# A transformer block (half feed-forward, attention, half feed-forward) on eight cores: two small jobs move from ScalarE to VectorE, and one dependency of the gate/up matmuls is split in two

## What is computed

```
x = x + 0.5 * ffn(layernorm(x))
x = x + attn(layernorm(x) * g + b)
x = x + 0.5 * ffn(layernorm(x))

ffn(x):  gate = x @ Wg.T;  up = x @ Wu.T          # 1024 -> 3072, int weights / 127
         return (silu(gate) * up) @ Wd.T          # 3072 -> 1024
attn(x): q, k, v = x @ Wq + bq, x @ Wk + bk, x @ Wv + bv   # 16 heads of 64
         w = softmax(q k^T / 8);  return w @ v
```

## Time and profile before

| | us |
|---|---|
| median of 2 runs | 4691.66 |
| the two runs | 4689.4 and 4693.92 |
| the profiled execution | 4682.5 |
| its span, slowest core (core 0) | 4681.0 |
| spans of the 8 cores | 4652.3 to 4681.0 |

### The profile page before, as it was taken

How to read it: one execution, slowest core, us unless ns; L and a number is a source line. 1 busy time by engine, 2 the same in 40 slices (tenths; PEclk the granted TensorE clock), 3 DMA queues, 4 the chain that set the end, 5 groups by cost and what they waited for, 6 DMA issues and landing times. The chain is left out here.

```text
span 4681.0 us, 55973 instructions; the slowest of 8 cores (4652.3 to 4681.0 us)
## 1 busy us (share of the span) xinstructions
PE 3372.0 (72%) x21982; PEld 1599.4 (34%) x22214; DVE 940.8 (20%) x1454; ACT 1504.1 (32%) x1864; POOL 145.0 (3%) x307
## 2 busy tenths in 40 slices
PE   0000997976866677589798897986876677579799
PEld 0000443432323343344343443432323344334344
DVE  1101113114320111121221212213330111131221
ACT  0001111101029999711110111101019999721110
POOL 1011000010000000000000000010000000000000
PEclk9999998987988998889899898997888988889899
DMA  8996232232000111123221232213000111033221
GB/s 226 207 260 168 69 121 80 56 80 73 9 18 1 37 37 37 65 63 117 81 72 73 72 117 81 72 48 87 28 18 1 37 37 37 23 95 117 81 73 44
DMA packets 344400, 353.90 MB, mean 76 GB/s; under 512 B 84552, under 2 KB 281160, under 8 KB 343120
## 3 DMA queue, kind: packets, MB, share of 16 engines
q1 hardware_dynamic: 238160, 230.74, 16.9%
q0 software_dynamic: 30976, 100.68, 6.8%
q10 hardware_dynamic: 75008, 18.88, 3.6%
HBM read 255.89 MB, written 88.08 MB: 73 GB/s over the span
## 5 line engine op out<-in xcount | busy, mean ns | idle before, releaser
L900 ACT ACTIVATE att_eS<-PS,cb 128x1024 bf16<-128x1024 f32 x1024 | 1051.1, 1132 | 32.8 <-PE PS L886 31.9
L886 PE MATMUL PS<-Q,K 64*128 64x512 bf16 x2048 | 431.7, 419 | 266.8 <-ACT att_eS L900 175.8
L818 PE MATMUL PS<-V,att_eS 128*128 128x65 bf16 x8192 | 373.2, 203 | 69.8 <-DVE att_x2b L849 69.8
L390 PE MATMUL PS<-ident,a1s_xntm 128*128 128x128 bf16 x256 | 32.4, 306 | 531.1 <-DVE a1s_xntm L377 531.1
L818 PEld LDWEIGHTS PS<-V,att_eS 128*128 128x128 bf16 x8192 | 312.7, 104 | 207.4 <-issue 207.4
L438 PE MATMUL PS<-cs_xnfm,cs_wslg 128*128 128x512 bf16 x1504 | 365.9, 384 | 7.1 <-DVE cs_xnfm L399 5.6
L438 PE MATMUL PS<-a1s_xnfm,a1s_wslg 128*128 128x512 bf16 x1504 | 365.6, 384 | 6.8 <-DVE a1s_xnfm L399 5.3
L444 PE MATMUL PS<-cs_xnfm,cs_wslu 128*128 128x512 bf16 x1504 | 363.0, 381 | 1.7
L444 PE MATMUL PS<-a1s_xnfm,a1s_wslu 128*128 128x512 bf16 x1504 | 362.0, 381 | 1.7
L482 PE MATMUL PS<-a1s_wdsb,a1s_hsb 128*128 128x512 bf16 x1504 | 332.2, 380 | 9.4 <-DVE a1s_hsb L461 7.8
L482 PE MATMUL PS<-cs_wdsb,cs_hsb 128*128 128x512 bf16 x1504 | 330.5, 379 | 9.2 <-DVE cs_hsb L461 7.5
(11 more groups left out here) (109 smaller groups left out, 2074.1 us busy)
## 6 DMA issues: line engine op xcount, KB each, us to landing
a1s_wslg<-wgT SPq DMA_DIRECT2D x48, 512.0 KB, 4.2
a1s_wslu<-wuT SPq DMA_DIRECT2D x48, 512.0 KB, 5.4
cs_wslg<-wgT SPq DMA_DIRECT2D x48, 512.0 KB, 4.1
cs_wslu<-wuT SPq DMA_DIRECT2D x48, 512.0 KB, 5.4
a1s_xst<-L_attn_x SPq DMA_DIRECT2D x32, 512.0 KB, 6.3
x1s<-a1s_xo POOLq DMA_DIRECT2D x32, 512.0 KB, 4.6
a2s_xst<-x1s SPq DMA_DIRECT2D x32, 512.0 KB, 3.4
att_x1q<-x1s SPq DMA_DIRECT2D x8, 2048.0 KB
```

Source lines behind the costliest of these rows:

```text
L390: inst = e.transpose(tview[:, dc * 128:(dc + 1) * 128], xntm[:, (tt % 2) * 1024 + dc * 128: (tt % 2) * 1024 + (dc + 1) * 128], ident[:])
L818: inst = e.matmul(PS1[:, (par * 2 + q2) * 512: (par * 2 + q2) * 512 + 65], expS[:, buf + kt * 1024 + par * 512 + qt * 128: buf + kt * 1024 ...
L886: inst = e.matmul(PS0[:, pp + par * 512: pp + (par + 1) * 512], K_sb[64 * par:64 * par + 64, hp * 2048 + r * 128: hp * 2048 + (r + 1) * 12 ...
L900: "scalar", lambda e, hp=hp, r=r, buf=buf, pp=pp: e.activation(expS[:, buf + r * 1024: buf + (r + 1) * 1024], PS0[:, pp:pp + 1024], AF.Exp ...
```

## The change

Three edits.

1. In `ffn_phase` the steps with th=0 wait for the fourth evacuation of the group, those with th=1 for the eighth, as all did before.
2. In `emit_norms` the 16 squares of a sequence are a product of the chunk with itself on VectorE instead of a Square on ScalarE.
3. In `attn_phase` the copy of the row sums is made by VectorE instead of ScalarE, and a drain is put ahead of the reciprocal that follows it on the same engine.

```diff
-                grp_ev = t_ev[g * 8 + 7]
+                grp_ev_h = {0: t_ev[g * 8 + 3], 1: t_ev[g * 8 + 7]}
...
                             t_mmgu = ph.op("tensor", gu_fn,
-                                           deps=[t_lg, t_lu, grp_ev,
+                                           deps=[t_lg, t_lu, grp_ev_h[th],
                                                  t_silu.get((g, k - 2)),
                                                  t_hmul.get((g, k - 2))],
...
-                t_sq[dc] = ph.op("scalar", lambda e, s=src_sb, dc=dc, sl=sl: e.activation(
+                t_sq[dc] = ph.op("vector", lambda e, s=src_sb, dc=dc, sl=sl: e.tensor_mul(
                     nsq[:, sl * 2048:(sl + 1) * 2048],
-                    s[:, dc * 2048:(dc + 1) * 2048], AF.Square),
+                    s[:, dc * 2048:(dc + 1) * 2048],
+                    s[:, dc * 2048:(dc + 1) * 2048]),
                     deps=[t_mm.get(dc - 2), t_red.get(pi - 1),
-                          t_sq.get(dc - 1)], inc="sc")
+                          t_sq.get(dc - 1)], inc="ev")
...
-                    t_l = ph.op("scalar", lambda e, qtp=qtp: e.copy(
+                    t_l = ph.op("vector", lambda e, qtp=qtp: e.tensor_copy(
                         lbuf[:, qtp * 4: qtp * 4 + 4][:, :, None],
                         PS1[:, :].rearrange("p (a t) -> p a t", a=4)[:, :, 64:65]),
-                        deps=pvdeps, inc="sc")
+                        deps=pvdeps, inc="ev")
                     t_r = ph.op("vector", lambda e, qtp=qtp: e.reciprocal(
                         lbuf[:, 8 + qtp * 4: 8 + qtp * 4 + 4],
-                        lbuf[:, qtp * 4: qtp * 4 + 4]), deps=[t_l], inc="ev")
+                        lbuf[:, qtp * 4: qtp * 4 + 4]),
+                        deps=[t_l], inc="ev", pre_drain=True)
```

## The result

| | before | changed |
|---|---|---|
| ratio of the times, changed to before | | 0.9877 (95% interval 0.9854 to 0.9901) |
| the same on the median shown of before, 4691.7 us | 4691.7 | 4634 (4623 to 4645) |
| two fastest runs, us | 4689.4, 4693.9 | 4634.7, 4638.6 |
| profiled execution, us | 4682.5 | 4621.2 |
| its mean span over the 8 cores, us | 4667.3 | 4599.2 |

The change makes the kernel 1.2% faster, 58 us (46 to 68); the forecast was 56 us, to 4636.

The account below looks back on a forecast made before the run. TensorE bounds the feed-forward stages, ScalarE the attention stages, dependent chains the short stages between. Gains 7 + 17 + 0 + 21 + 12 - 1 = 56 us take 4691.7 to 4636 us, range 4614 to 4668.

Parts of the forecast that it names:

- part 1: Feed-forward gate/up start: no wait for the eighth evacuation, 8 groups x 0.9 us, 7 us gained (3.5 to 10.6).
- if the clock rises at the same moment as before, an earlier start is worth half: Lower end for the gate/up start: matmuls run at the lower clock level, leaving 3.5 us gained.
- Part 2: Norms: squares on VectorE at 1.22 us each, a half falls from 17.26 to 12.96 us, 17 us gained.
- Rival A: Norms: the bf16 product runs at the f32 rate, 12 us lost instead of 17 gained, 4665 us; chance 0.08.
- The table load: Norms: one ScalarE load of 1.30 us leaves the start, one enters ahead of the square root; 0 gained.
- Part 3: Attention: row-sum copy on VectorE, 21 us from ScalarE's queue, 12 from shorter waits, 1 lost beside the residual adds.
- The slots: Attention: ScalarE's queue without the copies, 122 x 0.17 us, 21 us gained.
- the waits: Attention: TensorE gets its PV chunk 0.6 us earlier, so ScalarE waits less at low clock; 12 us gained (0 to 25).
- B: Attention: low-clock stretches end with the gap the copy makes, all 25 us of short waits go, 4623 us; chance 0.12.
- C: Attention: ScalarE's freed time is not used because TensorE then paces, 4668 us; chance 0.11.
- D: Attention: VectorE's chain makes TensorE, then ScalarE, wait at every chunk pair; at a 2.3 us chain 4718 us; chance 0.03.
- Up to 1.73 costs nothing: Attention: a VectorE chain up to 1.73 us makes no ScalarE wait; beyond it each us costs 124 us.

Follow-up runs that it names:

- The filled gap: Kernel before plus three unread matmuls ahead of each group's first gate matmul, old dependency kept: ratio 0.9976 (0.9961 to 0.999).
- part 1 by itself: Kernel before with only the split dependency of the gate/up steps: ratio 0.9983 (0.9946 to 1.002), profiled execution 4666.45 us.
- the last: Changed kernel with first gate/up step among the transposes, reciprocal straight out of PSUM and squares on both engines: ratio 0.9774, runs 4573 to 4579 us.

## Why the prediction came out as it did

**The total and the step that failed.** The total came out close, 58 us measured (46 to 68) against 56, and the change is within 2%, as forecast. It was made of three terms, of which two had about the right size. The third, part 1, is the step that failed: it was forecast at 7 us and measured 15. By the stage times the three add up to 66 us, so a total that fits within 2 us is partly luck.

**Part 1, forecast 7 us, measured 15, above its upper end of 10.6.** What goes is the wait for the eighth evacuation, as the text said; the term was mis-sized in two steps. The first took the gap as 0.9 from the recorded end of the transposes; the next matmuls can start before that end, so 1.22 went. The second was "if the clock rises at the same moment as before, an earlier start is worth half": the clock was let in only as something that lowers the gain. The filled gap shows that the moment moves with the pause, from 5.7 to 2.8 us after the transposes, which is worth 1.36 us a group; part 1 moves it as far (2.9), and as its matmuls also start earlier and so more of them at the low clock, 0.65 a group is left.

**Part 2, forecast 17 us, measured 18 (14.5 by the ratio).** The price of 1.22 for a product not seen before, got by halving the f32 product's part above the fixed 0.16, met 1.225. The Trainium skill (VectorE: DVE Perf Modes, the perf-mode tier table) has 1224 ns for it; the trace agrees. Rival A falls with it. The half for Q came out at 12.62, the one for K at 13.17, where more selector matmuls found the low clock. The table load moved as forecast and cost nothing on balance; the Trainium skill (ScalarE: Activation LUTs, What ACT_TABLE_LOAD costs) counts about 2.66 us with a drain, and the rows have a load of 1.28 from 1393.42 with nothing of a drain to be seen behind it, the root starts at 1394.71. That "by the page's figure the change would give back 1.4 us in each sequence" didn't follow: one load leaves and one enters, at whichever price, and the balance is 0 either way.

**Part 3, forecast 32 us, measured 33.** The slots gave 18 of 21, the waits 14 of 12. The chain was 1.27 against 1.29. One of the things that the text asked the profile to show was misstated, the reciprocal "about 0.9 after the PV chunk's end": by the text's own terms it is 0.44, and it is 0.41 (1480.71 to 1481.12). The text asked for a waiting time near 19 us and it is 15 to 16.

**The rivals.** B (all of the short waits go) and C (the freed time is not used) both fall: the waits went by half. D had half of the mechanism and the wrong price. The chain did not reach its threshold, but a long chain is dearer than stated: at 1.80 it cost 29 to 33 us, where D's reckoning gives 0.07 x 124 = 9, and at 2.59 twice what it gives. "Up to 1.73 costs nothing" asked when ScalarE is late at the high clock, and there it holds nearly. What it left out is that TensorE already waits when its chunk is late against its own place (1.35), and that with those waits the time at the low clock grows, where ScalarE's waits arise. At 1.80 all of part 3 is given back. So a slot freed on ScalarE with a chain about as long as before's brings next to nothing.

**Left open.** Why part 1 by itself measures 8 us by the ratio and 15 by its stage can't be told apart from scatter: its interval reaches from 25 us gained to 9 lost. How much of part 3's halved waits is the clock and how much the earlier chunk wasn't separated by a run; by the table the time at the low clock fell by 28% (225 to 162), and the waits for each us of it by 30% (0.123 to 0.086), so the two seem to share it. Which pauses of TensorE make the clock fall in attention wasn't tested beyond the length of the chain.

## What to carry to other kernels

A pause of TensorE ahead of a dense stretch cost its length here and the delayed rise of the clock behind it; where a dependency can't be loosened, put independent matmuls that are wanted anyway into the pause. Taking an operation off the engine that paces a loop paid here only while the chain in which it lands stayed shorter than the slack of the engine that feeds the loop, so measure that slack in the trace, as the time from the end of one chunk to the place where the next would stand without the chain. Where the waits of a stage come at a low clock, price the clock as part of the wait and in both directions.

## What the hardware did that was not expected

- Three matmuls that nobody reads, put into a pause of TensorE, made the kernel before faster by 0.24% (0.1 to 0.39%).
- Longer waits of TensorE in the attention stage bring further ones through the clock: 1.3 us more of chain took the granted clock of the same stretch of time from 0.92 to 0.58, and the stages of exponentials, with the same work in them, from 1051 to 1260 us.
- The recorded time of one exponential grows as the stage gets faster, 1132 ns in before, 1197 in the changed kernel, 1236 in the last, while the busy time of the group falls from 1051 to 1032 us and the spacing without copies is 1.005: neighbours overlap in the records, and only the spacing tells the rate.
- A copy of 128x4 out of PSUM costs VectorE 162 ns, and a pair of copies that wait for one another on ScalarE 0.17 and 0.25 us of its stream.
